# Two projections of the next chunk but one in the middle of a slot, key and query products ahead of the state's, scaled keys in ScalarE's gaps

## The reference

```python
mixed = jax.nn.silu(causal_conv4(x @ W_qkv))         # q, k, v, four taps per channel
z, a, b = x @ W_z, x @ W_a, x @ W_b
beta = jax.nn.sigmoid(b)
g = -jnp.exp(A_log) * jax.nn.softplus(a + dt_bias)
q = _l2norm(q) * DK ** (-0.5); k = _l2norm(k)
def step(S, inp):
    qt, kt, vt, gt, bt = inp
    S = S * jnp.exp(gt)[..., None, None]
    pred = jnp.einsum('bhk,bhkv->bhv', kt, S)
    u = (vt - pred) * bt[..., None]
    S = S + jnp.einsum('bhk,bhv->bhkv', kt, u)
    o = jnp.einsum('bhk,bhkv->bhv', qt, S)
    return (S, o)
# then an RMS norm of o, a gate with silu(z), and the product with W_out
```

## Time and profile before

| what | value |
|---|---|
| runs | 4840.66, 4842.49, 4827.86 us; median 4840.66 |
| the profiled execution | 4831.96 us, its span 4830.2 us |
| TensorE matmuls busy | 4403.5 us, 91% of the span |
| TensorE weight loads busy | 3615.9 us, 75% |
| VectorE busy | 3866.0 us, 80% |
| ScalarE busy | 2975.3 us, 62% |
| GpSimd busy | 1012.1 us, 21% |
| mean granted clock of TensorE | 0.964 of full speed |
| attention stages | about 741 to 2430 and 3108 to 4820 us |

### The profile page before, as it was taken

The page is one execution under the profiler, slowest core; times in us unless marked ns, Lnnn a source line. Parts: engine busy times, 40 slices in busy tenths (PEclk is TensorE's granted clock), DMA queues, the critical chain, the costliest instruction groups (busy, mean ns, idle before and its releaser), DMA issues. The chain is left out here.

```text
span 4830.2 us, 93590 instructions
## 1 busy us (share of the span) xinstructions
PE 4403.5 (91%) x32596; PEld 3615.9 (75%) x32596; DVE 3866.0 (80%) x8126; ACT 2975.3 (62%) x9834; POOL 1012.1 (21%) x1252
## 2 busy tenths in 40 slices
PE   5899939999999999999959998399999999999998
PEld 3578827888888888888845877388888888888887
DVE  6938988888888888888841599788888888888886
ACT  1146626777777777777711665366766667676665
POOL 0024411222212121212200344012121212121211
PEclk8999969999999999999979999699999999999999
DMA  1035642222222222223210566222222222222222
GB/s 56 30 91 174 189 137 70 82 75 83 78 83 75 80 83 77 82 78 82 63 31 11 154 182 194 77 76 83 76 74 81 78 81 81 75 85 74 76 76 64
DMA packets 580414, 422.57 MB, mean 87 GB/s; under 512 B 392808, under 2 KB 476312, under 8 KB 579502
## 3 DMA queue, kind: packets, MB, share of 16 engines
q1 hardware_dynamic: 563566, 408.20, 28.9%
q0 software_dynamic: 16384, 8.42, 1.1%
HBM read 296.24 MB, written 120.16 MB: 86 GB/s over the span
## 5 line engine op out<-in xcount | busy, mean ns | idle before, releaser
L1228 DVE SCALAR_TENSOR_TENSOR conv_l<-mix_l,taps_l,conv_l 128x512 f32<-128x512 f32 x1152 | 861.1, 757 | 156.0 <-ACT conv_l L1051 125.5
L854 PE MATMUL pj_l<-x_high,w_high_l 128*128 128x512 f32 x1280 | 572.7, 447 | 159.5 <-ACT w_high_l L1060 159.5
L1431 POOL TENSOR_TENSOR fac_l<-den_l,powers 128x4 f32<-128x4 f32 x256 | 258.9, 1012 | 1596.9 <-DVE den_l L1352 1595.3
L1196 ACT ACTIVATE Z_l<-gb_l 128x128 f32<-128x128 f32 x1024 | 266.6, 290 | 490.9 <-PE gb_l L1014 490.9
L854 PE MATMUL pj_l<-x_high,w_low_l 128*128 128x512 f32 x1280 | 519.0, 405 | 16.9 <-DVE W_l L1316 16.7
L854 PE MATMUL pj_l<-x_low,w_high_l 128*128 128x512 f32 x1280 | 512.8, 401 | 0.0
L637 POOL DMA_DIRECT2D own_dram<-key_kkS_l x512 | 298.2, 589 | 915.5 <-ACT key_kkS_l L509 905.3
L1023 PE MATMUL gb_l<-wo_l,gT_l 128*128 128x256 f32 x2048 | 480.0, 384 | 0.0
L1023 PEld LDWEIGHTS gb_l<-wo_l,gT_l 128*128 128x128 f32 x2048 | 372.6, 190 | 69.7 <-ACT Z_l L1196 25.6
L1362 DVE SCALAR_TENSOR_TENSOR x<-gb_l,fac_l,x 128x256 f32<-128x256 f32 x1024 | 412.9, 476 | 11.4 <-POOL fac_l L1431 0.2
L854 PEld LDWEIGHTS pj_l<-x_high,w_high_l 128*128 128x128 f32 x1280 | 242.5, 189 | 217.5 <-ACT w_high_l L1060 159.9
(11 more groups left out here) (204 smaller groups left out, 10773.9 us busy)
## 6 DMA issues: line engine op xcount, KB each, us to landing
rows_l<-rows_dram SPq DMA_DIRECT2D x128, 1024.0 KB, 5.6
k_dram<-kT_l SPq DMA_DIRECT2D x128, 256.0 KB, 2.3
kk_dram<-key_kkS_l SPq DMA_DIRECT2D x128, 256.0 KB, 2.3
kq_l<-k_dram SPq DMA_DIRECT2D x128, 256.0 KB, 3.3
kkS_l<-kk_dram SPq DMA_DIRECT2D x128, 256.0 KB, 5.8
w_raw_l<-in_wx SPq DMA_DIRECT2D x32, 640.0 KB
lane_k_l<-own_dram SPq DMA_DIRECT2D x32, 512.0 KB, 4.1
t_dram<-lane_t_l SPq DMA_DIRECT2D x14, 1024.0 KB, 4.9
```

Of the source, the lines that this page charges most:

```text
L854: ins = nc.tensor.matmul(pj_bank(c, t), wt[:, k, t, :], xt[:, k, :, at], start=(k == 0 and n == 0), stop=(k == KD - 1 and n == 2))
L1196: ins = nc.scalar.activation(Z[:, g, bank(b)], gb[:, 0, g, bank(b)], ACT.Square, accum_out=ss_o[:, g, b:b + 1])
L1228: ins = nc.vector.scalar_tensor_tensor(out, mix[:, t, :, i:i + P], wt(i), out, ALU.mult, ALU.add)
L1431: nc.gpsimd.tensor_tensor(fac[:, g, :], den[:, g, :], m.powers[:, 1, :], ALU.pow).then_inc(fac_ok[g], 1)
```

## The change

- On TensorE the projections of the next chunk inside the slot move up by one: t = 2, 3 and 4 stand where 1, 2 and 3 stood, and the place between L954 and the state products (L965), where t = 4 stood, holds no projection. Two projections (t = 0 and 1) of the next chunk but one follow the output products, where there was one.
- For c > 0 the key and query product stands directly behind L954, ahead of the state products. For c = 0 it keeps its place behind L954, but without the projection between.
- On ScalarE `copy_z32` opens the slot. The scaled keys of c = 1 and 2 move behind the value copies of their slot; those of c = 0 into the slot before (c = 3). The two copies of the early projections move to the slot's end, ahead of the output squares; the copy of t = 2 and the first gate move forward.
- `ktok` becomes two buffers, and `square_keys` waits for older scaled keys than before.

```diff
--- before.py
+++ after.py
@@ -674,7 +674,7 @@
         sq_kq = diag_b[:, :, :].rearrange("p g n -> p (g n)")
         decay = sb("decay", [P, GROUPS, WIDE])
         ap = sb("ap", [P, 2, GROUPS, BATCH, 2, P])
-        ktok = sb("ktok", [P, WIDE])
+        ktok = sb("ktok", [P, 2, WIDE])
         ke = sb("ke", [P, GROUPS, WIDE])
         vn = sb("vn", [P, GROUPS, WIDE])
         qd = sb("qd", [P, GROUPS, BATCH, P])
@@ -912,7 +912,7 @@
                             ins = nc.tensor.matmul(gb[half(g), 1, 0, part(b)], ap[:, c % 2, g, b, 0, 0:HALF],
                                                    Te[:, g, b, :], start=True, stop=True)
                     ins.then_inc(z32_mm, 1)
-                    fill(1)
+                    fill(2)
                     pe.wait_ge(xd_in, 64 * (it + 1))
                     pe.wait_ge(z32_cp, it + 1)
                     if not first:
@@ -925,12 +925,12 @@
                     ins.then_inc(dx_mm, 1)
                     if not last:
                         keys_token_major(nh, ncn, False)
-                        project(nh, ncn, 2, 0, False)
-                        project(nh, ncn, 2, 1, False, (0, 1))
+                        project(nh, ncn, 3, 0, False)
+                        project(nh, ncn, 3, 1, False, (0, 1))
                     pe.wait_ge(w_blocks_in, 64 * (it + 1))
                     pe.wait_ge(w_up, 4 * (it + 1))
                     if not last:
-                        project(nh, ncn, 2, 1, False, (2,))
+                        project(nh, ncn, 3, 1, False, (2,))
                     for b in range(BATCH):
                         for g in range(GROUPS):
                             ins = nc.tensor.transpose(gb[:, 1, g, part(b)], W[half(g), b, :], eye[half(g), half(g)])
@@ -942,7 +942,7 @@
                                                    W[half(g), b, 0:HALF], start=True, stop=True)
                             if b == BATCH - 1:
                                 ins.then_inc(z64_mm[g], 1)
-                    fill(3)
+                    fill(4)
                     if not last:
                         queries_token_major(nh, ncn, False)
                     pe.wait_ge(x_in, 32 * (it + 1))
@@ -955,7 +955,8 @@
                                                    X[HALF:, g, b * P + HALF:(b + 1) * P], start=True, stop=True)
                             if b == BATCH - 1:
                                 ins.then_inc(x64_mm[g], 1)
-                    fill(4)
+                    if not last and c > 0:
+                        key_products(nh, ncn)
 
                     if c > 0:
                         for g in range(GROUPS):
@@ -971,7 +972,7 @@
 
                                 nc.tensor.matmul(gb[:, 1, g, bank(b)], S[:, c % 2, g, bank(b)], qd[:, g, b, :],
                                                  start=(b == 0), stop=False, skip_group_check=True)
-                    if not last:
+                    if not last and c == 0:
                         key_products(nh, ncn)
                     for g in range(GROUPS):
                         if c > 0:
@@ -997,8 +998,9 @@
                                                    start=(c == 0), stop=True, skip_group_check=True)
                         ins.then_inc(o_mm[g], 1)
                     if it < KHEADS * CHUNKS - 2:
-                        project(*following(nh, ncn), 0, 0, False)
-                        project(*following(nh, ncn), 0, 1, False)
+                        for t in range(2):
+                            project(*following(nh, ncn), t, 0, False)
+                            project(*following(nh, ncn), t, 1, False)
                     if not last:
                         values_token_major(nh, ncn)
                     for g in range(GROUPS):
@@ -1031,8 +1033,9 @@
                 keys_token_major(0, 0, True)
                 queries_token_major(0, 0, True)
                 key_products(0, 0)
-                project(0, 1, 0, 0, False)
-                project(0, 1, 0, 1, False)
+                for t in range(2):
+                    project(0, 1, t, 0, False)
+                    project(0, 1, t, 1, False)
                 values_token_major(0, 0)
                 steps(body)
 
@@ -1084,8 +1087,8 @@
                     q = 4 * h + c
                     act.wait_ge(ktok_mm, q + 1)
                     if not first:
-                        act.wait_ge(ke_ok, 6 * h + 2 * c)
-                    nc.scalar.activation(ktok[:, :], kk[:, 0, :], ACT.Copy).then_inc(ktok_cp, 1)
+                        act.wait_ge(ke_ok, 6 * h + 2 * max(0, c - 1))
+                    nc.scalar.activation(ktok[:, q % 2, :], kk[:, 0, :], ACT.Copy).then_inc(ktok_cp, 1)
                     square(0).then_inc(k_sq, 1)
 
                 def square_queries(h, c):
@@ -1110,7 +1113,7 @@
                     act.wait_ge(decay_ok, 2 * q + g + 1)
                     for b in range(BATCH):
                         last = decay[:, g, (b + 1) * P - 1:(b + 1) * P]
-                        ins = nc.scalar.activation(ke[:, g, bank(b)], ktok[:, bank(b)], ACT.Copy, scale=last)
+                        ins = nc.scalar.activation(ke[:, g, bank(b)], ktok[:, q % 2, bank(b)], ACT.Copy, scale=last)
                     ins.then_inc(ke_ok, 1)
 
                 def copy_z32(it):
@@ -1148,22 +1151,15 @@
                 def body(h, c, first, last):
                     it = 4 * h + c
                     nh, ncn = following(h, c)
-                    if c < CHUNKS - 1:
-                        scaled_keys(h, c, 0)
+                    copy_z32(it)
                     if not last:
-                        copy_mix(nh, ncn, 0, False)
-                    copy_z32(it)
-                    if c < CHUNKS - 1:
-                        scaled_keys(h, c, 1)
-                    if not last:
-                        copy_mix(nh, ncn, 1, False)
+                        copy_mix(nh, ncn, 2, False)
                         square_keys(nh, ncn, False)
                         silu_conv(nh, ncn, 0)
+                        silu_z(nh, ncn, 0)
                     copy_right(it)
                     for g in range(GROUPS):
                         copy_z(g, it)
-                    if not last:
-                        copy_mix(nh, ncn, 2, False)
                     copy_left(it)
                     if c == 2 and h < KHEADS - 1:
                         for t in range(CONVS):
@@ -1171,7 +1167,6 @@
                     if c > 0:
                         copy_corner(it)
                     if not last:
-                        silu_z(nh, ncn, 0)
                         square_queries(nh, ncn)
                     if c == 0:
                         copy_corner(it)
@@ -1179,6 +1174,9 @@
                         silu_z(nh, ncn, 1)
                         for t in range(1, CONVS):
                             silu_conv(nh, ncn, t)
+                    if 0 < c < CHUNKS - 1:
+                        for g in range(GROUPS):
+                            scaled_keys(h, c, g)
                     if c == 2 and h < KHEADS - 1:
                         for t in range(CONVS, PROJS):
                             split_weights(h + 1, t)
@@ -1190,6 +1188,12 @@
                         for g in range(GROUPS):
                             act.wait_ge(o_mm[g], it + 1)
                             nc.scalar.activation(oT[:, g, :], gb[:, 1, g, :], ACT.Copy).then_inc(o_cp[g], 1)
+                    if c == CHUNKS - 1 and not last:
+                        for g in range(GROUPS):
+                            scaled_keys(nh, ncn, g)
+                    if it < KHEADS * CHUNKS - 2:
+                        for t in range(2):
+                            copy_mix(*following(nh, ncn), t, False)
                     for g in range(GROUPS):
                         act.wait_ge(sso_mm[g], it + 1)
                         for b in range(BATCH):
@@ -1211,6 +1215,10 @@
                 square_keys(0, 0, True)
                 square_queries(0, 0)
                 scaled_values(0, 0)
+                for g in range(GROUPS):
+                    scaled_keys(0, 0, g)
+                for t in range(2):
+                    copy_mix(0, 1, t, False)
                 steps(body)
 
             @block.vector
```

## The result

| kernel | median us (runs) | span of the profiled execution | mean granted clock |
|---|---|---|---|
| before | 4839.26 (4) | 4830.2 | 0.964 |
| after | 5083.33 (4) | 5080.3 | 0.937 |

The change makes the kernel slower: ratio 1.0507, interval 1.0488 to 1.0526, +244 us. I had forecast 4970, so the direction was right and the size was not: 5083 lies 43 us above the upper end of my range.

The account below looks back on a forecast made before the run. It took TensorE's program, run back to back plus a few waits, to bound the attention slots. Waits removed and added summed to +137 us on 4831.96, forecast 4970 us, 80% range 4900 to 5040.

Parts of the forecast that it names:

- (a): Slot start, c=0 to 2: L923's 0.62 us wait for ScalarE's copy vanishes in 96 slots, -59.5 us.
- (b): Value and output turns in c=2: VectorE gets a projection's time, so the slots' surplus over c=1 goes, -33.6 us.
- (c): Weight loads waiting for VectorE's masked products: a third of 20.9 us goes, -7 us, bounds 0 and -20.9.
- (d): From L923 to the turn of W (L936): the 0.40 us wait for VectorE's W mostly stays, +1 us.
- (e): Behind L954, c>0: L883 waits 2.11 us for ScalarE's corner copies, then squares; with slower restart 94 x 2.21, +207.7 us.
- (f): Before L883 in c=0: without the covering projection it waits 0.70 us for squares, 0.11 before; +18.9 us.
- (g): Slot end, layer 0's c=3: scaled keys and projection copies make ScalarE's output squares 0.65 us late, 15 times, +9.8 us.
- (h): c=1 and 2: VectorE's decay scan waits for the later scaled keys, covered by its update, 0 us.
- The sum: All wait terms added: +137 us on the profiled execution's 4831.96 us, 4969, forecast as 4970 us.
- The clock: TensorE's 94 new 2.1 us gaps cost no clock, judged by a harmless 1.36 us gap in the key stage.
- rival D: The clock falls after the new gap before L883: +190 us more, +327 or more in all, from 5160 us; chance 0.04.

Follow-up runs that it names:

- x4: The kernel before with only ScalarE's scaled keys moved as in the change and `ktok` in two buffers; 4769.57 us, ratio 0.9864.
- x1: The changed kernel with four extra matmuls that nothing reads between L954 and L883 for c>0; 4956.81 us, ratio 1.0250.
- y1: The kernel before with only the key and query product put ahead of the state products for c>0; 4941.63 us, ratio 1.0220.
- x2: The changed kernel with one extra matmul that nothing reads between L954 and L883 for c>0; 5007.3 us, ratio 1.0354.

## Why the prediction was right or wrong

**(a), the first wait: right.** L923 starts 2.22 us into the slot, as forecast, and x4 shows that the move of the scaled keys alone brings it. There a c=0 slot gains 1.13 us, more than this wait, because the second wait and the short one before L883 shrink with it.

**(b), VectorE's surplus in c=2: right.** In x1, where the clock holds, a c=2 slot takes 29.2 us in both layers, as a c=1 slot does; in after every c=2 slot is slowed and takes 30.8, as a slowed c=1 slot does. **(c), the masked products: right.** The row of the weight loads fell by 17 us, all in c=3 slots. From start to start, from the slot's last projection to the output turn, those took 2.58 us where c=1 took 2.38; in after both take 3.8, with one projection more. So the waits were worth 32 x 0.2, some 6 us, and I had taken 7.

**(d), the second wait: right.** L923 to L936 is 2.91 us in c=1 against the unhindered 2.61 of the earlier trace rows: 0.30 stays, and c=3 now has it too. In c=0 only 0.15 stays, so the term was some 5 us too high.

**(e), the wait before L883: right to the hundredth.** Forecast 2.72 us after L954's start; measured 1130.90 to 1133.62 and 3631.56 to 3634.28. The next group follows 0.99 later, as forecast. The waits view's 217.6 us are 94 x 2.04 + 32 x 0.62 = 212, and the rest at the stages' starts. In c=2 ScalarE's weight splits did not add to it: they ended just as the corner copies could begin, 0.71 us behind L954's start.

**(f): right in its start.** In c=0 L883 starts 1.31 us behind L954 (1106.61 to 1107.92), idle 0.62.

**(g): right.** In layer 0's c=3 the output product waits 0.72 us for the squares (forecast 0.65); the waits view has 10.8 us in 15 (forecast 9.8).

**(h): right.** Nothing on TensorE waits for work behind the scaled keys.

**The sum.** With the wait filled and the clock at 1.00 (x1) the kernel is 120 us above before; my sum was +137. x1's slots came out 24.1, 29.2, 29.2 and 28.2 (27.4 in layer 1) against 24.3, 29.2, 29.2 and 28.1 (27.5). The slots that I listed and my sum did not agree with each other: 16 heads of two layers with the listed slots are about 123 us above before, not 137. So as a forecast of the waits, 4970 was 13 us too high.

**What failed is the step called "The clock".** It read "a gap of that size cost no clock", from an idle time of 1.36 us in the key stage, put the cost of the clock in the sum at nothing, and gave rival D 0.04 and a price of 190 us, outside the range. What the runs showed in its place is a cost of 127 us: 80 of the 94 waits brought the clock down, for some 1.6 us each. The sign that the prediction had named for being wrong is there too, a clock below 1 in the attention stages:

```profile
790.00:2415.00 1625.00, 1518.48 (x12300) 1300.95 (x12300) 1277.32 (x2868) 1136.76 (x3945) 311.81 (x322) 0.96 0.26 73
```

The gap that this edit makes is not of the size of the key stage's: it is 2.04 us, half as long again, and it recurs in three slots of four. But the step was weaker than that. The key stages of before idled for 1.3 to 1.4 us eight times without a fall, some 45 us apart, and y1 idled for 1.7 us in 30 slots without one, while behind L954 in x2 1.41 us was enough in 29 slots of 94. So a gap that did no harm at one place of the program did not vouch for a gap at another, not even for one of its own size. What makes the place behind L954 the worse one these runs don't show.

The kind of price that D had was right (190, from 94 x 2; 127 measured). With that added to my sum, the forecast would have been 5097 against 5083. I had weighed D as unlikely for want of a row, where the want of a row called for a wider range.

The Trainium skill's page "TensorE: Matmul & The Clock Gate", section "HAM oscillation — how this bites in real kernels", tells of a kernel in which a wait on every tile puts the engine back to half clock each time; this trace agrees in 80 of 94 slots. By the rule in the same section of the Trainium skill only longer idle gaps than these matter; here 2.04 us was enough and even 1.41 in part, and the measurement decides.

## What to carry to other kernels

Before moving work out of the place between a product and what reads its result, list what the next matmul on TensorE needs from other engines, in their program order: the order of one pair on ScalarE was worth 242 us here. Price each recurring idle time on TensorE twice, once as a wait and once as a fall of the clock behind it; when the trace shows harmless gaps of nearly that size only at other places of the program, let the range hold the fall. And test the parts of a change one by one: a part worth -67 us was hidden in a whole worth +244.

## What the runs showed of the hardware that I had not expected

An idle time of 2.04 us on TensorE behind L954 brought the granted clock to 1.2 GHz 80 times in 94, one of 1.41 us 29 times in 94, one of 0.97 us never. With equal waits of 2.04 us all slots with c=2 and c=3 were slowed and 18 of 32 with c=1. One of 1.7 us behind a projection, in y1, did it in none of 30. Each fall cost 1.6 to 1.7 us, nearly as much as the wait that caused it. Matmuls without use in the wait took 127 us off the kernel, and two were as good as four (4959 and 4957 us). After the product the low clock shows in that product's own row or only in the group behind it: the product group's row reads 1.78 us in the slot at 3506.27 and 1.16 in others that are slowed right after.
